# Six stage openings written in another order in a twelve-stage fp32 transformer kernel

## The reference, cut to what matters

```
for l in 0..3:
    x = x + tanh(g_xattn[l]) * mixer_l(layernorm(x), ctx)
    x = x + tanh(g_ffn[l])   * ffn_l(layernorm(x))

mixer_0: a scan over the 64 tokens with decay 0.9
ffn_0:   a transformer block (4-head attention), then 8 experts, top 1, capped
mixer_1: a similarity matrix of x and ctx, softmax both ways
ffn_1:   16 experts, top 4 out of 2 chosen groups
mixer_2: 16-head cross-attention, 64 x 64 mask:
    score = where(mask == 0, -1e9, q k^T / sqrt(8));  softmax(score) v w_o^T + b_o
ffn_2:   8 experts, top 2, routed by a normalized row
mixer_3: the same attention with a key padding mask (-inf), then an encoder tail:
    y = LN(q + attn);  LN(y + gelu(y W1 + b1) W2 + b2)
ffn_3:   soft decision tree of depth 8 (255 gates, 256 leaves)
```

## Time and profile before

| | |
|---|---|
| three runs | 2944.06, 2941.98, 2934.96 us |
| median | 2941.98 us |
| profiled execution | 2939.39 us, its span 2937.6 us |
| granted TensorE clock over the span | 0.847 |
| PE | busy 2278.6 us, 78% of the span |
| DVE | 1834.6 us, 62% |
| ACT | 1197.1 us, 41% |
| POOL | 1169.0 us, 40% |
| HBM | 43 GB/s over the span |

### The profile page before, as it was taken

One profiled execution on the slowest core, in us unless ns is written; L12 is line 12 of the kernel. 1 busy time (PEld: TensorE's weight loads), 2 busy tenths in 40 slices (PEclk: granted clock), 3 DMA queues, 4 the chain that ended last, 5 costly groups with the idle time before them and its releaser, 6 DMA issues. The chain is left out here.

```text
span 2937.6 us, 59647 instructions
## 1 busy us (share of the span) xinstructions
PE 2278.6 (78%) x20218; PEld 1766.0 (60%) x20218; DVE 1834.6 (62%) x5797; ACT 1197.1 (41%) x2400; POOL 1169.0 (40%) x1364
## 2 busy tenths in 40 slices
PE   4788799597639999975888885099954888879676
PEld 1555522286538888863665664099952665658665
DVE  7688577688756666654876666200013777864588
ACT  1666244244313333324654442044322555645332
POOL 4455178423441111113334435533325555435611
PEclk6788799797769999986987776599986899989888
DMA  6200011422010000012001100122221111000001
GB/s 205 94 16 20 33 40 51 130 76 60 25 51 24 24 23 24 23 35 89 25 27 32 32 23 28 45 65 72 70 64 40 33 35 34 25 10 2 7 25 32
DMA packets 153438, 129.78 MB, mean 44 GB/s; under 512 B 18996, under 2 KB 131390, under 8 KB 152392
## 3 DMA queue, kind: packets, MB, share of 16 engines
q1 hardware_dynamic: 130120, 92.31, 10.5%
q0 software_dynamic: 12288, 25.45, 2.9%
q10 hardware_dynamic: 10752, 8.39, 0.9%
HBM read 79.99 MB, written 46.10 MB: 43 GB/s over the span
## 5 line engine op out<-in xcount | busy, mean ns | idle before, releaser
L1822 PE MATMUL scores<-l1ffn_x_t,l1ffn_w 128*128 128x256 f32 x888 | 230.6, 383 | 0.0
L1787 POOL COPY l1ffn_w<-l_w_ahead 128x1032 f32 x74 | 75.2, 1046 | 347.5 <-DVE l1ffn_hid L1895 339.8
L1910 DVE SCALAR_TENSOR_TENSOR l1ffn_acc<-bank,l1ffn_xs,l1ffn_acc 128x128 f32<-128x128 f32 x518 | 157.9, 346 | 71.6 <-PE bank L1834 66.3
L2576 ACT ACTIVATE l_probs_t<-bank 128x512 f32<-128x512 f32 x256 | 141.0, 596 | 120.8 <-PE bank L237 113.8
L2644 DVE TENSOR_REDUCE l_top<-scores 128x16 f32<-128x1024 f32 x128 | 155.3, 1213 | 55.3 <-DMA l1mix_ctx<-in_ctx 31.6
L1834 PEld LDWEIGHTS bank<-l_w_ahead,l1ffn_hid 128*128 128x128 f32 x1184 | 178.3, 191 | 15.4 <-issue 0.3
L1834 PE MATMUL bank<-l_w_ahead,l1ffn_hid 128*128 x1184 | 179.6, 274 | 0.1
L3023 DVE COPY l2ffn_y<-bank 128x512 f32<-128x512 f32 x34 | 23.5, 690 | 242.7 <-PE bank L2928 242.7
L237 PEld LDWEIGHTS bank<-ident,l_probs 128*128 128x128 f32 x1024 | 139.3, 162 | 56.5 <-issue 39.4
L2504 PE MATMUL bank<-l_v_blocks,l_probs_t 128*64 128x18 f32 x4096 | 157.6, 221 | 19.9 <-issue 18.2
L2504 PEld LDWEIGHTS bank<-l_v_blocks,l_probs_t 128*64 128x64 f32 x4096 | 146.9, 151 | 35.1 <-issue 32.1
(11 more groups left out here) (497 smaller groups left out, 5833.1 us busy)
## 6 DMA issues: line engine op xcount, KB each, us to landing
l2ffn_xs<-scratch_l_in SPq DMA_DIRECT2D x136, 64.0 KB, 1.8
scratch_l_out<-l2ffn_y SPq DMA_DIRECT2D x34, 256.0 KB, 2.3
x_all<-scratch_x SPq DMA_DIRECT2D x32, 256.0 KB, 4.6
l_ctx_t<-in_ctx_t SPq DMA_DIRECT2D x32, 256.0 KB
l_w_ahead<-in_l_w SPq DMA_DIRECT2D x3, 2048.0 KB, 12.9
l1ffn_xs<-scratch_l_in SPq DMA_DIRECT2D x37, 136.0 KB, 2.2
scratch_l_out<-l1ffn_acc SPq DMA_DIRECT2D x37, 128.0 KB, 1.8
x_all<-in_x SPq DMA_DIRECT2D x16, 256.0 KB, 5.9
```

What stands on the lines that cost most here:

```text
L1822: mm = pe.matmul(bank[1 + m % HB][:, part * TP:(part + 1) * TP], w13[:, j % WR, k, c:c + P], x_t[:, j % 2], start=True, stop=True)
L1910: v.scalar_tensor_tensor(out=acc[:, j % 2, t, :], in0=bank[5 + p % 2][:, c:c + D], scalar=xs[:, j % RING, t, D + e:D + e + 1], in1=acc[:, ...
L2576: act.activation(probs_t[:, n % RT, half * 4:half * 4 + 4].rearrange("p a q -> p (a q)"), bank[4 + half][:, :], ACT.Identity).then_inc(p_t ...
```

## The change

Six openings are written in another order. No computation is added or removed.

- `l0_attention`: SP issues the load of x group 0 ahead of the seven constants. DVE makes the statistics of group 0, then the two spread biases, then z of group 0, then the output bias, then group 1. POOL waits for the output bias behind the first root, not at its start.
- `l1_mix`: SP issues x of groups 0 and 1 ahead of the five constants. DVE waits for the constants behind the normalization of group 0.
- `cross_attention` (both layers): POOL gathers group 0 first, then writes zeros and ones into `v_blocks`, and waits for the bias behind the four gathers. DVE makes bias, flags and router constants behind z of group 0 (`make_bias`, the new `vector_finish`). `shift(0)` stands ahead of the joining of group 2.
- `l3_mlp`: w1 has a semaphore of its own. ACT fetches y of two groups before it splits w1; PE turns y of group 0 before it waits for w1's low part; DVE scales the affine constants behind the first low part of y.
- `l3_tree`: DVE normalizes group 0 before it copies the two merged weights out.

The diff, cut to its core:

```diff
 l0_attention, SP
+                sp.dma_start(x_all[:, 0:G, :], x1_dram[:, 0:G, :]).then_inc(x_in[0], DMA)
                 for dst, name in ((wqkv, "l0_wqkv"), (wo, "l0_wo"), (b_cols, "l0_b_cols"), (bo, "l0_bo"),
                                   (ln_g, "l0_ln1_g"), (ln_b, "l0_ln1_b"), (wg, "l0_wg")):
                     sp.dma_start(dst[:, :], dram[name]).then_inc(w_in, DMA)
-                for g in range(GROUPS):
+                for g in range(1, GROUPS):
 POOL
-                pool.wait_ge(w_in, 7 * DMA)
-                pool.wait_ge(bias_done, 1)
...
                     root(0, g)
+                    if g == 0:
+                        pool.wait_ge(bias_done, 1)
                     add_bias(g)
 DVE
-                for g in range(2):
-                    x_stats(g)
-                    norm_x(g)
+                x_stats(0)
+                spread_biases()
+                norm_x(0)
+                add_bv()
+                x_stats(1)
+                norm_x(1)
 l1_mix, SP
+                for g in range(2):
+                    sp.dma_start(group_of(x_all, g), group_of(x2_dram, g)).then_inc(x_in[g], DMA)
                 for dst, name in ((w_sim[:, :], "l1_w_sim"), (b_sim[:, :], "l1_b_sim"), (wqv[:, :, :], "l1_wqv"),
...
 DVE
                     apply(i, h)
+                    v.wait_ge(w_in, 5 * DMA)
+                    v.wait_ge(zeroed, 1)
+                    route.vector_setup(v)
                     make_key(i, h)
 cross_attention, POOL
-                pool.memset(v_blocks[:, :, :, :, :], 0.0).then_inc(blocks_set, 1)
...
-                pool.wait_ge(bias_done, 1)
                 for i in range(4):
                     for which in range(G):
                         gather(i, which)
+                    if i == 0:
+                        pool.memset(v_blocks[:, :, :, :, :], 0.0).then_inc(blocks_set, 1)
+                        pool.wait_ge(blocks_set, 1)
...
+                        route.pool_setup(pool)
                     if i < 2:
                         ln.pool_rstd(pool, i)
+                pool.wait_ge(bias_done, 1)
 DVE
-                v.wait_ge(blocks_set, 3)
...
                     joined.vector(v, i)
                     stats(i)
                     apply(i)
+                    if i == 0:
+                        make_bias()
+                        mask.vector_finish(v)
+                        tail.vector_setup(v)
+                        route.vector_setup(v)
+                shift(0)
                 joined.vector(v, 2)
-                shift(0)
 PaddingMask
+    def vector_finish(self, v):
         v.tensor_reduce(self.flags[:, :], self.mask[:, :].rearrange("p (t k) -> p t k", k=S), AX.X, ALU.min)\
 l3_mlp, ACT
                     fetch(0, 0)
                     fetch(1, 1)
+                    act.wait_ge(w1_in, DMA)
+                    act.activation(w1_high[:, :], w1[:, :], ACT.Identity).then_inc(w_high_done, 1)
                     y_out(i, h)
+                    act.wait_ge(w_in, 5 * DMA)
 DVE
+                    v.wait_ge(w_high_done, 1)
+                    v.tensor_tensor(w1_low[:, :], w1[:, :], w1_high[:, :].bitcast(F32), ALU.subtract)\
+                        .then_inc(w_low_done, 1)
+                    y_rest(i, h)
+                    v.wait_ge(w_in, 5 * DMA)
+                    v.tensor_scalar(ln_g[:, :], ln_g[:, :], tanh_g, None, ALU.mult).then_inc(affine, 1)
 l3_tree, DVE
-                    for g in range(2):
-                        stats(g)
-                        apply(g, g)
+                    stats(0)
+                    apply(0, 0)
+                    keep_merged()
+                    stats(1)
+                    apply(1, 1)
```

More of the change, by code:

```diff
@@ L2379, in _ @@
             def _(pool):
-                pool.memset(v_blocks[:, :, :, :, :], 0.0).then_inc(blocks_set, 1)
-                pool.wait_ge(blocks_set, 1)
-                for j2 in range(2):
-                    pool.memset(v_blocks[half_rows(j2), :, :, :, 2 * HD + j2], 1.0).then_inc(blocks_set, 1)
-                pool.wait_ge(blocks_set, 3)
-                route.pool_setup(pool)
                 parts = G * joined.picks.K if joins is not AsItIs else 0
@@ L2404, in _ @@
                         gather(i, which)
+                    if i == 0:
+                        pool.memset(v_blocks[:, :, :, :, :], 0.0).then_inc(blocks_set, 1)
+                        pool.wait_ge(blocks_set, 1)
+                        for j2 in range(2):
+                            pool.memset(v_blocks[half_rows(j2), :, :, :, 2 * HD + j2], 1.0).then_inc(blocks_set, 1)
+                        pool.wait_ge(blocks_set, 3)
+                        route.pool_setup(pool)
                     if i < 2:
                         ln.pool_rstd(pool, i)
+                pool.wait_ge(bias_done, 1)
                 over_tiles(slot)
@@ L2624, in _, with make_bias @@
                 mask.vector_setup(v)
-                tail.vector_setup(v)
-                route.vector_setup(v)
-                v.wait_ge(bv_made, 1)
-                v.tensor_tensor(bias[:, :], bank[6][:, 0:D], bo[:, :], ALU.add).then_inc(bias_done, 1)
-                v.wait_ge(bias_done, 1)
+                def make_bias():
+                    v.wait_ge(bv_made, 1)
+                    v.tensor_tensor(bias[:, :], bank[6][:, 0:D], bo[:, :], ALU.add).then_inc(bias_done, 1)
+                    v.wait_ge(bias_done, 1)
                 def stats(i):
@@ L3109, in _ @@
             def _(sp):
-                for dst, name in ((w1[:, :], "l3_w1"), (w2[:, :, :], "l3_w2"), (b1[:, :], "l3_b1"),
+                sp.dma_start(w1[:, :], dram["l3_w1"]).then_inc(w1_in, DMA)
+                for dst, name in ((w2[:, :, :], "l3_w2"), (b1[:, :], "l3_b1"),
                                   (b2[:, :], "l3_b2"), (ln_g[:, :], "l3_ln2_g"), (ln_b[:, :], "l3_ln2_b")):
@@ L3115, in _ @@
             def _(pool):
-                pool.wait_ge(w_in, 6 * DMA)
+                pool.wait_ge(w_in, 5 * DMA)
                 pool.wait_ge(affine, 2)
@@ L3166, in main, with front @@
                     ago(i, 1, lambda g: outputs(g, 1 - h))
-                over_lagging(turn_y, main, pe, 3)
+                def front(i, h):
+                    turn_y(i, h)
+                    pe.wait_ge(w_low_done, 1)
+                    pe.wait_ge(w_in, 5 * DMA)
+                over_lagging(front, main, pe, 3)
             @block.scalar
             def _(act):
-                act.wait_ge(w_in, 6 * DMA)
-                act.activation(w1_high[:, :], w1[:, :], ACT.Identity).then_inc(w_high_done, 1)
                 def fetch(i, h):
```

46 lines of the change are left out of this document (21 added, 25 removed).

## The result

The changed kernel takes 2900.22 us (median of 4 runs, 2897.73 to 2902.51), the kernel before 2943.02 us beside it. The ratio is 0.9851 with a 95% interval of 0.9832 to 0.9871, so 43.9 us are gone (38 to 49). The profiled execution has a span of 2897.0 us, 40.6 less than before. The page's busy times have moved by 5.5 us at most, and the counts of instructions not at all: the work is the same.

The account below looks back on a forecast made before the run. Chains of PE, DVE and POOL, begun anew behind each barrier, were taken to set the time; 18.4+14.0+4.3+4.0+3.0+2.7 = 46.4 us, and 2939.4-46.4+2.6 = 2895.6 us, own range 2884 to 2907, wider 2880 to 2919.

Parts of the forecast that it names:

- rivals 1 and 3: 1: POOL's gathers bind both attention stages, 2899.3 us, chance 0.23; 3: DVE locks out POOL in layer 3's opening, 2898.9, 0.05.
- What bounds the kernel: Whole kernel: no engine fills the run; chains of PE, DVE and POOL, begun anew behind each barrier, set the time.
- Layer 3, first join: Layer 3's attention: gather 0 starts without waiting for the bias, so the first join comes 17.3 us earlier.
- Layer 3, the stall: Layer 3: DVE's 12.11 us wait for PE's scores moves along unchanged; shift(0) ahead of group 2's join adds 1.1 us.
- Layer 2: Layer 2's attention: first join 16.3 us earlier, second 11.4 to 16.2 beside the large load; term 14.0 us.
- Cover: Layer 3's attention: 6.0 us of DVE's flags and small work hide in the wait for gather 1.
- l3_mlp: l3_mlp opening: w1's low part takes 0.7 us, first hidden product 3.4 to 4.5 us earlier; term 4.3 us.
- l3_tree: l3_tree opening: first z is ready before the merged products, so PE's transpose follows the copies; term 4.0 us.
- l0_attention: l0_attention opening: x group 0 issued first, 3.23 us earlier, z still behind the spread biases; term 3.0 us.
- l1_mix: l1_mix opening: x issued 2.27 us earlier and no longer behind the constants' traffic; term 2.7 us.
- Rival 2: All stages: work not begun with the opening gives half the gain back, 23.2 us remain, 2918.8 us; chance 0.12.
- Rival 4: Attention loops: more stalls of 12.11 us from late PE signals, with five more 2956 us, slower; chance 0.03.

Follow-up runs that it names:

- The change's two halves: Kernel before with only both cross_attention openings changed, 2913.38 us; changed kernel with both cross_attention openings put back, 2928.85 us.
- experiment 5: Changed kernel with POOL's memsets of v_blocks behind the gather of group 1 instead of group 0, both attention stages: 2896.39 us.
- experiment 6: Changed kernel with layer 3's flags ahead of the first join again and layer 2's join of group 2 ahead of the first maximum: 2908.06 us.
- experiment 7: Changed kernel with 10 unused PE transposes in l3_mlp behind the transpose of y of group 1: 2898.90 us.
- Experiments 4 and 8: Changed kernel with gathers three groups ahead instead of four, 2930.95 us; changed kernel with groups 3 and 4's gathers in four portions behind row maxima, 2896.58 us.
- the paced kernel: Changed kernel with the gathers of groups 3 and 4 in four portions, each behind a row maximum, third root ahead: 2896.58 us.

## Why the prediction came out

Time, sign and range were right. That the sum came within 5 us is in part luck: by the means layer 2 gave 3.2 us more than its term and layer 3 3.7 less. The time alone doesn't pick the forecast either, since rivals 1 and 3 had put 2899.3 and 2898.9 us, nearer to the 2900.22 than 2895.6; the stages have to tell them apart. Step by step:

- **What bounds the kernel**: right in the main. `l3_tree` and layer 2's attention moved by about what their first z or join moved or more, the others by less, and `l1_mix` by nothing that can be seen. By the prediction's own sign ("if a stage as a whole shrinks by clearly less than its first join, statistics or z moved") it was wrong there. The change's two halves, in runs of their own, gave 32.7 and 15.3 us (forecast 32.4 and 14.0).
- **Layer 3, first join**: forecast 13.2 us after the start, measured 14.65. The term missed what POOL does to DVE. The prediction's third rival looked for the reverse, DVE's mask table holding up POOL's gathers. That wasn't put to the test: the last gather of group 0 ended at 2170.16, and the table began at 2170.78. Beside DVE's memset of 1.76 us a gather kept its 0.95. It was POOL's memset, moved into DVE's way, that cost 1.3 us (13.37 without it, experiment 5).
- **Layer 3, the stall**: "I expect the stall to move along with it" was right, 14.65 us for 12.11. The 1.1 us added for `shift(0)` weren't there: the first maximum came 23.9 us earlier in the stage, and that of group 1 only 16.0, because the stall took the rest. By the rows the stall is longer because it now comes behind the statistics of group 2: POOL goes from its twenty gathers straight on to that group's root and four gathers more, where before the root waited until DVE had gone on. The root before, then root and next gather of the changed kernel:

```profile
2260.27 0.23 POOL L204 TENSOR_SCALAR l_ln_var_eps<-l_ln_mv 128x4 f32<-128x4 f32 x1 [7.23 <-DVE l_ln_mv L200]
```

```profile
2221.59 0.24 POOL L204 TENSOR_SCALAR l_ln_var_eps<-l_ln_mv 128x4 f32<-128x4 f32 x1
2223.16 1.09 POOL L1940 DMA_INDIRECT l_gathered<-scratch_l_out,l_slot  x1 [0.20 <-issue]
```

  This step failed in size: 18.4 forecast, 14.7 over all traces. The 18.6 of the pair is chance, since from the third group to the twelfth the lead is 13.8 to 14.6 us and the rest comes in the last groups.
- **Layer 2**: the first join 14.7 us earlier, forecast 16.3. POOL's memset (1.88 us for 0.22) has 0.3 us of that; more lies in gather 0 itself, which with the memset out of the way took 7.45 us to the join (1305.17 to 1312.62 in experiment 5) and not 6.47. Rival 1's collision took place almost in full: gather 1 took 10.75 us. It started only 1.91 us ahead of the load's issue (1320.23, 1322.14) where the prediction had 3.9, and the second join came 10.4 us earlier, below the lower bound of 11.4. SP's eight stores of zeros lie beside it too, as they did before, and no run parts the two. But it bound nothing, though only just: z of group 1 was ready at 1335.83, and PE, released by ACT's values of group 0, turned it at 1336.20:

```profile
1334.71 1.12 DVE L212 TENSOR_SCALAR l_z<-x_all,l_ln_mv,l_ln_rstd 128x128 f32<-128x128 f32 x4 [1.60 <-POOL l_ln_rstd L206]
1336.20 1.09 PE L237 MATMUL bank<-ident,l_z 128*128 128x128 f32 x4 [1.43 <-ACT l_v_blocks L2590]
```

  So the stage followed the first join, 15.0 us at the second group. The middle of two joins was the wrong way to take the term: 14.0, at most 16.3, for 15.6 in the pair and 17.2 over all traces, of which some is scatter.
- **Cover**: right. Flags and constants were hidden, and experiment 6 shows what they cost without (4.9 us at the join).
- **l3_mlp**: the mechanism came in to 0.1 us (first hidden product 4.6 us earlier, forecast 4.5), but the stage gained 2.3 in the pair and 2.7 in the mean. The clock, which the prediction left out, took 2 us back: it fell between 13 and 18 us, behind a wait of PE of 2.07 us, and with that gap filled it didn't (experiment 7).
- **l3_tree**: right, 4.1 and 3.9.
- **l0_attention**: x came in as forecast (2.82 us after the start), and z of group 0 came 3.4 us earlier in the stage. The mean gives 2.6 us for the stage, but with the same code it scatters from 272.4 to 278.7 us, and the later the clock rose, the longer it was. Between traces with a like clock some 2 us are left, an estimate: the old order took 275.9 and 276.5 us where the clock reached 1.00 at 15 and 16 us, the new one 273.6 and 274.8 where it did so at 13 and 18. That the pair shows a loss is chance.
- **l1_mix**: x came in as forecast (2.97 us) and the first key was 2.7 us earlier in the stage, but the stage isn't shown to be shorter: the kernel before took 301.5 and 302.2 us, the ten traces of the new order 301.5 to 303.9. By DVE's sixteen keys, one a group, the lead in the pair is 1.8 to 3.1 us through thirteen groups, 1.7 at the next two and 0.6 at the last. So the term of 2.7 was given back within the stage. PE's clock is the likely reason and isn't shown, since no run held it up there. Two stretches of 6 us, from 168 us after the start, in the kernel before and in the changed kernel (columns as above):

```profile
720.52:726.52 6.00, 1.48 (x10) 1.06 (x8) 5.62 (x25) 3.50 (x9) 4.18 (x7) 0.82 0.00 1
726.52:732.52 6.00, 5.10 (x49) 4.60 (x48) 5.66 (x14) 1.96 (x5) 3.04 (x3) 0.61 0.15 49
```

```profile
721.17:727.17 6.00, 3.32 (x15) 2.92 (x16) 5.66 (x20) 3.38 (x9) 4.18 (x7) 0.53 0.06 20
727.17:733.17 6.00, 5.24 (x48) 4.74 (x47) 5.48 (x19) 1.08 (x2) 1.77 (x2) 0.50 0.10 30
```

- **Rival 2** (gain given back within the stages): in small parts, 2 us in `l3_mlp` by the clock and the 2.7 of `l1_mix`, not the half. **Rival 4** (more stalls): no; there is still one large one, 2.5 us longer.

What stays open: why PE's signals and products are late while POOL issues gathers. Experiments 4 and 8 show that it follows the run, but not what inside the chip ties the two. Why the attention stages scatter by 4 to 6 us with the same code isn't settled either, nor what takes back the gain of `l1_mix`.

## What to carry to other kernels

Where stages end in barriers, sort each opening by who needs what first, and let nothing that the first gather or load doesn't use stand ahead of it on its queue; the gain is then about what the first join moves, less what later waits and the clock take back. When work moves to another place, ask what will run beside it there, as POOL's memset did beside DVE's mask table. Before a gain or loss of a few us in one stage is put down to the change, compare the granted clock there, and a second trace of the same code.

## What the runs showed of the hardware

- PE's signals come late while POOL issues a long run of indirect gathers: scores done at 2216.91 by the trace reached DVE at 2230.69, and in the paced kernel small products came out with up to 1.74 us between them. With a shorter run the wait of 14.65 us became 0.98.
- The granted clock of the same code rises at different times: in seven traces of the changed `l0_attention` it reached 1.00 between 12 and 25 us after the stage's start, and the stage's length followed (272.4 to 278.7 us).
- PE's clock could be held at 1.00 by 10 unused transposes in a gap of 2.07 us (`l3_mlp`, 132.4 for 134.3 us).
- A POOL memset of 2.03 us stretched a DVE operation from 0.22 to 1.88 us, while gathers beside DVE's memset kept their 0.95 us.
